# Routing the first 20 of 32 token tiles inside the attention stage ahead of each expert stage

## What is computed

```python
x = x + jnp.tanh(g_xattn[0]) * _L0_xattn_ref(_layernorm(x), ctx, ...)        # softmax attention, 8 heads
x = x + jnp.tanh(g_ffn[0])   * _L0_ffn_ref(_layernorm(x), ...)               # 8 experts, 2 per token, hidden 128
x = x + jnp.tanh(g_xattn[1]) * _L1_xattn_ref(_layernorm(x), ctx, ctx, ...)   # linear attention, 16 heads
x = x + jnp.tanh(g_ffn[1])   * _L1_ffn_ref(_layernorm(x), ...)               # a causal block, 32 heads, then
#   h = _rms(x, ff_ln_w); topv, topi = top_k(h @ wg, 4); gate = softmax(topv)  16 experts, 4 per token, hidden 256
#   y_e = (silu(h @ w1[e]) * (h @ w3[e])) @ w2[e];  x + sum over the chosen e of gate_e * y_e
```

## Time and profile before

| | us |
|---|---|
| median of 3 runs | 3075.64 |
| lowest, highest | 3073.47, 3088.97 |
| profiled execution | 3069.99 |
| its span | 3068.2 |
| its granted TensorE clock, mean share of full speed | 0.86 |
| busy in the span: TensorE, VectorE, ScalarE, GpSimd | 2334.5, 1909.9, 1086.7, 1091.4 |

### The profile page before, as it was taken

The page is one execution under the profiler, slowest core; times in us unless marked ns, Lnnn a source line. Parts: engine busy times, 40 slices in busy tenths (PEclk is TensorE's granted clock), DMA queues, the critical chain, the costliest instruction groups (busy, mean ns, idle before and its releaser), DMA issues. The chain is left out here.

```text
span 3068.2 us, 57408 instructions
## 1 busy us (share of the span) xinstructions
PE 2334.5 (76%) x19856; PEld 1800.8 (59%) x19856; DVE 1909.9 (62%) x3797; ACT 1086.7 (35%) x2118; POOL 1091.4 (36%) x1088
## 2 busy tenths in 40 slices
PE   4888899863782598993788898889886316999991
PEld 3455555443671487882576677667675315888770
DVE  4788788634453477774677867777775612444574
ACT  1566666521340232322333333333332202333330
POOL 2455455325325000000444443434442476000366
PEclk9898878655896799996999999899998557999995
DMA  5555655223566211103332232232223344333575
GB/s 104 112 134 126 126 131 117 44 79 99 161 183 182 90 35 52 38 27 104 77 76 62 62 78 64 62 75 66 56 73 102 117 156 149 99 99 99 179 232 158
DMA packets 251153, 313.43 MB, mean 102 GB/s; under 512 B 43648, under 2 KB 205568, under 8 KB 249728
## 3 DMA queue, kind: packets, MB, share of 16 engines
q1 hardware_dynamic: 190272, 220.09, 26.9%
q0 software_dynamic: 26624, 58.79, 7.3%
q10 hardware_dynamic: 33984, 30.95, 3.0%
HBM read 126.93 MB, written 98.30 MB: 73 GB/s over the span
## 5 line engine op out<-in xcount | busy, mean ns | idle before, releaser
L1655 POOL TENSOR_TENSOR ca_qk<-ca_qk,ca_q_swap 128x512 f32<-128x512 f32 x160 | 233.3, 1458 | 504.8 <-DVE ca_q_swap L1799 504.8
L317 DVE TENSOR_REDUCE soft_top<-soft_pa 128x4 fp32r<-128x1024 f32 x256 | 311.7, 1218 | 125.0 <-PE soft_pa L387 124.7
L738 POOL DMA_INDIRECT moe_yg<-moe_ys_rows,moe_slot_id x192 | 193.4, 1007 | 474.6 <-DMA moe_ys_rows<-moe_ys 364.1
L237 ACT ACTIVATE soft_prob<-soft_pb 128x1024 f32<-128x1024 f32 x256 | 262.0, 1023 | 230.2 <-PE soft_pb L371 229.9
L726 POOL DMA_INDIRECT moe_rows<-moe_hn,moe_slot_id x192 | 200.8, 1046 | 123.5 <-DVE moe_slot_id L911 65.5
L1870 PE MATMUL ca_pp<-ca_ht_hi,ca_w_hi 128*128 128x512 f32 x320 | 151.4, 473 | 97.5 <-ACT ca_q_f L1691 76.2
L1057 PE MATMUL moe_pgu<-moe_w_hi,moe_xt_hi 128*128 x472 | 192.8, 409 | 31.4 <-DVE moe_xt_lo L971 28.3
L1073 PE MATMUL moe_py<-moe_w_d,moe_at 128*128 x788 | 211.8, 384 | 0.0
L1691 ACT ACTIVATE ca_q_f<-ca_pp 128x512 f32<-128x512 f32 x160 | 94.9, 593 | 308.6 <-PE ca_pp L1870 301.1
L976 DVE TENSOR_TENSOR moe_act_f<-moe_silu,moe_pgu 128x256 f32<-128x256 f32 (+1 forms) x236 | 88.7, 376 | 172.7 <-ACT moe_silu L791 171.5
L971 DVE TENSOR_TENSOR moe_xt_lo<-moe_pt,moe_xt_hi 128x256 fp32r<-128x256 f32 x236 | 99.9, 423 | 138.9 <-ACT moe_xt_hi L786 138.7
(11 more groups left out here) (246 smaller groups left out, 6402.8 us busy)
## 6 DMA issues: line engine op xcount, KB each, us to landing
ca_q_swap<-ca_q_f SPq DMA_DIRECT2D x640, 64.0 KB, 2.0
moe_xs<-moe_rows SPq DMA_DIRECT2D x236, 128.0 KB, 2.0
moe_ys_rows<-moe_ys ACTq DMA_DIRECT2D x236, 128.0 KB
soft_rep<-soft_parts SPq DMA_DIRECT2D x384, 64.0 KB
moe_rows<-soft_blank SPq DMA_DIRECT2D x27, 768.0 KB
moe_hn<-scratch SPq DMA_DIRECT2D x16, 512.0 KB, 6.6
moe_xd<-scratch SPq DMA_DIRECT2D x64, 128.0 KB, 2.7
ca_vs<-ca_v SPq DMA_DIRECT2D x16, 512.0 KB
```

Source lines behind the costliest of these rows:

```text
L237: act.activation(prob[:, k % 4, :, :], p_b[:].rearrange("p (h s) -> p h s", h=2), ACT.Exp).then_inc(prob_ready, 1)
L317: dve.tensor_reduce(heads[:, j:j + 2, :, g], p_a[:].rearrange("p (h c s) -> p h c s", h=2, c=HALF), AX, ALU.max).then_inc(a_done, 1)
L738: pool.indirect_dma_start(out=yg[:, t % 2, k, :], out_offset=None, in_=ys_rows[h], in_offset=bass.IndirectOffsetOnAxis(ap=slot_id[:, t, k: ...
L1655: pool.tensor_tensor(qk[:, u % 2, m, :], qk[:, u % 2, m, :], q_swap[:, p % 2, :], ALU.add).then_inc(qk_ready, 1)
```

## The change

MOE_TILES = (20, 12) replaces COUNT = (24, 8). A new class `Router` holds the routing of one part, with a method for each engine's share. Part 0's twenty tiles are routed in the attention stage ahead, one tile after the other in softmax attention and chunk by chunk in causal attention: `spread` (VectorE, statistics), `root` (GpSimd), `scale` (VectorE; ScalarE in causal attention), `turn` (TensorE, transposes) and `keep_turned` (ScalarE), `grade` (TensorE, router products) and `keep_scores` (ScalarE), `choose` (VectorE). When all twenty are graded, `tally`, `rank`, `keep_ranks`, `place`, `map_blocks`, `keep_map`, `exps` and `weigh` run once, and `send` issues the scatters, 6 a pass in softmax attention from pass 28 on (40 in all) and 5 a step in causal attention from step 50 on (80 in all). Slots, weights and block experts go through DRAM to the expert stage (`leave`, `finish`), which routes the other twelve tiles itself and makes the low parts of weights in between. The norm's weight is folded into the router and, for the second stage, into the experts' high and low parts instead of the rows. TensorE's blocks wait for the tables as well; part 0's first block has no scatter to wait for. Blocks: 47 + 31 = 78 and 95 + 63 = 158.

Causal attention keeps `ht_hi`/`ht_lo`, `v`/`vs` and `ot_hi`/`ot_lo` once instead of twice: values are projected in places 0 and 1 of their own chunk, and ScalarE overwrites `ot_hi` only when the output products of the step before have been made. In softmax attention `xo` has four buffers instead of two.

The core of the diff:

```diff
+MOE_TILES = (20, 12)
...
+class Router:
...
+    def load(self, sp):
...
+    def spread(self, dve, g, row):
+        stats, mv, var = self.stats, self.mv, self.var
+        for t in range(self.GRP):
+            dve.bn_stats(stats[:, t, :], row(self.GRP * g + t)).then_inc(self.stat, self.stat_ticks.one())
...
+        for t in range(self.GRP):
+            dve.bn_aggr(mv[:, t, :], stats[:, t, :]).then_inc(self.stat, self.stat_ticks.one())
...
+    def root(self, pool, g):
...
+        pool.tensor_tensor(self.rstd[:], self.var[:], self.half_neg[:], ALU.pow).then_inc(self.rstd_ready, 1)
...
+    def scale(self, eng, g, row):
...
+        for i in range(self.GRP):
...
+    def turn(self, pe, first, tiles, out, ident):
+        pe.wait_ge(self.row_ready, first + tiles)
+        for t in range(tiles):
+            for k in range(self.KC):
+                mm = pe.transpose(out[:, t * DIM + k * PART:t * DIM + (k + 1) * PART],
+                                  self.rows[:, first + t, k * PART:(k + 1) * PART], ident)
...
+    def keep_turned(self, act, n, src, ht):
...
+    def grade(self, pe, g, tiles, out, ht):
...
+                mm = pe.matmul(out[:, t * self.EXPERTS:(t + 1) * self.EXPERTS], ht[:, t * DIM + k * PART:t * DIM + (k + 1) * PART],
+                               self.router[:, k, :], start=(k == 0), stop=(k == self.KC - 1))
...
+    def keep_scores(self, act, g, tiles, src):
...
+    def choose(self, dve, first, tiles, graded):
...
+            dve.max(top8[:, t, :], self.score[:, t, 0:E]).then_inc(route, ticks.one())
...
+            dve.match_replace(self.left[:, t, :], top8[:, t, :], self.score[:, t, :], MARK).then_inc(route, ticks.one())
...
+    def tally(self, dve):
...
+    def rank(self, pe, out):
...
+    def keep_ranks(self, act, src):
...
+    def place(self, dve):
...
+    def map_blocks(self, pe, out, ident):
...
+    def exps(self, act, stretches):
...
+    def weigh(self, dve):
...
+    def send(self, pool, first, last):
+        to = self.c["moe_rows"][self.h]
+        if first == 0:
+            pool.wait_ge(self.idx_ready, 1)
+        for n in range(first, min(last, self.n * self.TOP)):
+            t, k = divmod(n, self.TOP)
+            pool.indirect_dma_start(
+                out=to, out_offset=bass.IndirectOffsetOnAxis(ap=self.slot[:, t, k:k + 1], axis=0),
+                in_=self.rows[:, t, :], in_offset=None, bounds_check=self.blocks * PART - 1, oob_is_err=False
+            ).then_inc(self.sent, 16)
+    def tables(self, nc):
...
+    def leave(self, sp):
...
+    def finish(self, sp):
+        sp.wait_ge(self.saved, 48)
+        sp.wait_ge(self.sent, 16 * self.n * self.TOP)
...
-CLEARS = (19, 8)
+CLEARS = (16, 11)
...
-    LOAD, RING = 4, 16
+    LOAD, RING, KEEP = 4, 16, 4
+    ROUTED, STRETCH, SENDS = MOE_TILES[0], 4, 6
...
-        y, xo = sb("y", [PART, 2, T]), sb("xo", [PART, 2, T])
+        y, xo = sb("y", [PART, 2, T]), sb("xo", [PART, KEEP, T])
...
+        RANK = ROUTED + 6
...
+                route.leave(sp)
...
+                        past(pool, route.row_ready, min(t - KEEP + 1, ROUTED))
...
+                    if routed(i - 4):
+                        route.root(pool, i - 4)
...
+                    if i > RANK + 1:
+                        if i == RANK + 2:
+                            pool.wait_ge(cleared[0], 16 * CLEARS[0])
+                        route.send(pool, SENDS * (i - RANK - 2), SENDS * (i - RANK - 1))
+                route.send(pool, SENDS * (TILES + 1 - RANK), 2 * ROUTED)
...
+                    if routed(i - 6):
+                        route.keep_scores(act, i - 6, 1, p_x[0][:, T:T + 8])
...
+                    if routed(i - 5):
+                        route.keep_turned(act, i - 5, p_x[0][:, 0:T], turned[:])
+                    if i == RANK:
+                        route.keep_ranks(act, p_x[0])
+                        route.exps(act, ROUTED // STRETCH)
+                    if i == RANK + 1:
+                        route.keep_map(act, p_x[0])
...
+                    if routed(i - 4):
+                        dve.wait_ge(xo_ready, i - 3)
+                        route.spread(dve, i - 4, lambda t: xo[:, t % KEEP, :])
                     maxima(i, 1)
...
                     maxima(i, 6)
+                    if routed(i - 4):
+                        route.scale(dve, i - 4, lambda t: xo[:, t % KEEP, :])
                     maxima(i, 7)
+                    if routed(i - 6) and (i - 5) % STRETCH == 0:
+                        route.choose(dve, i - 5 - STRETCH, STRETCH, i - 5)
+                    if i == RANK - 1:
+                        route.tally(dve)
+                    if i == RANK + 1:
+                        route.place(dve)
+                    if i == RANK + 3:
+                        route.weigh(dve)
...
                     values(i - 1, 3)
+                    if routed(i - 6):
+                        route.grade(pe, i - 6, 1, p_x[0][:, T:T + 8], turned)
...
                     score(i, 7)
+                    if routed(i - 5) or i in (RANK, RANK + 1):
...
+                    if routed(i - 5):
+                        route.turn(pe, i - 5, 1, p_x[0], ident_f[:])
+                    if i == RANK:
+                        route.rank(pe, p_x[0])
+                    if i == RANK + 1:
+                        route.map_blocks(pe, p_x[0], ident_f)
                     values(i, 2)
...
-    COUNT = (24, 8)
+    COUNT = MOE_TILES
...
+        new = slice(FIRST[1], TILES)
+        route = Router(nc, st, name, name, 1, c, EXPERTS, TOP, norm, GRP, slot_id[:, new, :], wk[:, new, :], expert_of[:, START[1]:], x_new)
...
+                for dst, src in zip((slot_id[:, 0:COUNT[0], :], wk[:, 0:COUNT[0], :], expert_of[:, 0:BLOCKS[0]]), c[name + "_tables"]):
...
-                    if n == 0:
-                        sp.wait_ge(sent[h], 16 * COUNT[h] * TOP)
+                    if b == START[1]:
+                        sp.wait_ge(route.sent, 16 * NEW * TOP)
...
+                route.send(pool, 0, NEW * TOP)
+                pool.wait_ge(table_in, 48)
+                pool.wait_ge(route.sent, 16 * NEW * TOP)
...
+                high(0)
+                high(1)
+                route.keep_ranks(act, p_gu[0])
+                high(2)
+                high(3)
+                route.keep_map(act, p_at[0])
+                route.exps(act, GROUPS)
+                for e in range(4, EXPERTS):
+                    high(e)
...
+                for g in range(GROUPS):
...
+                    route.choose(dve, GRP * g, GRP, g + 1)
+                route.tally(dve)
+                low(0)
+                low(1)
+                route.place(dve)
+                low(2)
+                low(3)
+                route.weigh(dve)
+                for e in range(4, EXPERTS):
+                    low(e)
+                if norm == "layer":
...
+                pe.wait_ge(const_in, 32)
+                for g in range(GROUPS):
+                    for i in range(2):
+                        past(pe, route.ht_ready, 2 * (g - 1) + i + 1)
+                        route.turn(pe, GRP * g + 2 * i, 2, p_t[i], ident[:])
+                    past(pe, route.score_out, g - 1)
+                    route.grade(pe, g, GRP, p_y[g % 2], ht)
+                route.rank(pe, p_gu[0])
+                route.map_blocks(pe, p_at[0], ident)
                 pe.wait_ge(wlo_ready, EXPERTS)
                 pe.wait_ge(down_in, 16 * EXPERTS)
-                pe.wait_ge(expert_ready, PARTS)
+                pe.wait_ge(table_in, 48)
...
-        ht_hi, ht_lo = (sb(n, [PART, 2, KC, CHUNK], fp32r) for n in ("ht_hi", "ht_lo"))
+        ht_hi, ht_lo = (sb(n, [PART, KC, CHUNK], fp32r) for n in ("ht_hi", "ht_lo"))
...
-        v, vs = (sb(n, [PART, 2, TPC, KVHEADS * HD]) for n in ("v", "vs"))
+        v, vs = (sb(n, [PART, TPC, KVHEADS * HD]) for n in ("v", "vs"))
...
-        ot_hi, ot_lo = (sb(n, [PART, 2, RQ, 2 * PART], fp32r) for n in ("ot_hi", "ot_lo"))
+        ot_hi, ot_lo = (sb(n, [PART, RQ, 2 * PART], fp32r) for n in ("ot_hi", "ot_lo"))
+        route = Router(nc, st, "ca", "moe1", 0, c, 16, 4, "rms", TPC)
...
+        ROUTED = MOE_TILES[0] // TPC
+        SENDS = 5
...
+        def routing(n, place):
+            ch, j = step_of(n)
+            return ch - 1 if j == place and 0 <= ch - 1 < ROUTED else None
...
+        RANK = SPC * (ROUTED + 1)
...
+                    r = routing(n, 5)
+                    if r is not None:
+                        route.root(pool, r)
...
+                    if n > RANK + 1:
+                        route.send(pool, SENDS * (n - RANK - 2), SENDS * (n - RANK - 1))
+                route.send(pool, SENDS * (STEPS + 2 - RANK - 2), 4 * MOE_TILES[0])
...
-                            past(act, y_ready, n - 2)
...
+                            past(act, y_ready, n - 1)
...
+                    r = routing(n, 5)
+                    if r is not None:
+                        route.scale(act, r, routed_row(r))
+                    r = routing(n, 6)
```

(46 more changed lines are left out.)

## The result

The changed kernel takes 3064.56 us (median of 6 runs, 3062.95 to 3073.06), and its ratio to the kernel before is 0.9958 (95% interval 0.9941 to 0.9975): faster by 0.4%, about 13 us, where I had forecast 24 us, 0.8%. The profiled execution took 3064.46 us, its span is 3062.7. The sign was right, the gain about half.

A forecast was written before the change was run, and what follows sets the result against it. Bound: serial expert openings (score, rank, scatter, load), and attention stages where TensorE and VectorE are late in turns. Softmax +60, first experts -66, causal +78, second experts -96: -24 us, median 3052 us, own range 3025 to 3078, overall 2985 to 3112.

The forecast's parts named there:

- Openings: Starts of the two expert stages before their first blocks: shorter by 69 us (129.3 to 60) and 104 us (to 103).
- Sums at the end: GpSimd's serial fetches behind the expert blocks: +8 us in the second stage, +3 us in the first.
- Softmax scatters: Sixteen scatters behind GpSimd's last product in softmax attention, 21 us, plus 3 us of that product's lateness: 24 us.
- Softmax iterations: Softmax attention: spread and choose add 1.25 us to each of 20 iterations, TensorE's work nothing: 25 us.
- upper bound of 45: Upper end for the work inserted into softmax iterations, with everything serial: 45 us.
- Single ot buffers: Causal attention: ScalarE's copy must wait for the previous step's output products: +15 us, between 0 and 30.
- Routed chunks: Causal attention: per-chunk routing work on VectorE and TensorE, 6.1 us in each of five chunks: 30 us (15 to 45).
- Ranking: Causal attention: rank, place and weigh once at full clock, 4.8 + 2 + 8.2: 15 us (8 to 20).
- Rival B: Insertions fall into idle time of both attention stages, saving 50 of the 138 us added: 3002 us; chance 0.25.
- Rival C: GpSimd becomes the bound of causal steps, scatters costing 1654 + 300 ns beside VectorE's products: 3100 us; chance 0.18.
- Rival D: Openings instead wait for low halves and down weights behind VectorE's ranking, 83 and 128 us: 3100 us; chance 0.12.
- The row against the page: Earlier trace: a scatter took 4.93 us beside VectorE weight subtractions, though the Trainium skill's rule implies no hold-up.

The follow-up runs named there:

- no_pe: Changed kernel without TensorE's transposes and router products (and ScalarE's keeping of them) in softmax attention; ScalarE copies eight features as scores: softmax stage 726.6 us against 740.2.
- no_dve: Changed kernel without VectorE's spread and scale and GpSimd's root in softmax attention; ScalarE copies the rows: softmax stage 727.7 us against 740.2.
- neither: Changed kernel with both TensorE's and VectorE's per-tile routing work left out of softmax attention: softmax stage 706.5 us against 740.2.
- single_buf: Kernel before with only the single ht, v, vs and ot buffers and moved values' products, nothing routed early: causal stage 949.1 us against 945.4.
- late_rank: Changed kernel with softmax attention and first expert stage as before, causal ranking one step later, six scatters a step: 3135.43 us, ratio 0.994 to before.

## Why the prediction was right in sign and about double in size

- Openings, right. -69 and -104 against -67.3 and -111. The first block waits for down weights and low halves, as said. The 7 us more in the second: the low halves were done 78 us after its start, not 82, and the sixteen down weights took SyncE 9.71 us to issue, not the 14.67 of the earlier trace rows.
- Sums at the end, right: +8 against +7.3, 48 fetches for 41; +3 against +0.9.
- Softmax scatters, right: 24 against 24.0. Its ranking: 11 against 12 (means of 84 and 72 in that phase).
- Softmax iterations, wrong: 25 against 42 (37 in 21 iterations, 5 in the next three; means of the repeated kernels). The step that failed is "of that I take nothing, since TensorE waits for the peaks' DMA right there". no_pe, no_dve and neither put TensorE's term at 11 to 15 us. An idle gap whose end is another engine's or a DMA's work, which itself stands in the same chain, moves with the chain and covers nothing. Spread and scale, 17 in my sum, cost 18 to 21; choose, 8, is in the 7 to 10 that neither keeps, with ScalarE's copies. The second thing at nothing in my sum is the granted clock, 0.77 instead of 0.86: by the estimate above 13 to 16 us, which lie inside these numbers. My upper bound of 45 would have held it all. (The 15.7 us that I gave for an iteration at full clock was a misreading: at 1.00 it took 16.97.)
- Causal attention: 78 against 82.2 (87 by repeated stages), from errors that cancel. Single ot buffers 15, measured 0 to 4, the moved values among it: VectorE's 18.2 us of the earlier trace rows was a sign of slack, which I read and then priced all the same. Start +3, measured -3 to -6, since the first values moved out of it. Routed chunks 30, measured 33 (35 by the means of the kernels). Ranking 15, measured 29 (139.0 without scatters, against 110). Step by step against single_buf the changed kernel is 14.2 us longer in step 48, 7.0 in step 49 (place) and 7.4 in step 51 (weigh). The first is the term that was mis-sized: 4.8 for ranks that took 8.9, 6.0 of them L241's work at full clock, and nothing for the 4.55 us in which TensorE waits for VectorE's tally. Scatters 15, measured 16.7.
- Linear attention, no term: -4.7, and in the eight kernels with early softmax routing 387.7 to 393.2, without it 391.7 to 401.2. It is not explained; the stage's code is the same.
- Rival B (insertions fall into idle time) is refuted in both stages, which grew by 77 and 87 and not by 50 less than my 138. Rival C's price did not come about; its mechanism showed at six scatters a step. Rival D is refuted by the openings of 62 and 96. The row against the page held in the second opening only: there a scatter again took 5.50 us beside eight weight subtractions of VectorE. These are the timelines of GpSimd and VectorE of the changed kernel, beside the earlier trace rows:

```profile
2504.11 5.50 POOL L326 DMA_INDIRECT moe_rows<-moe_x_new,moe_slot_id  x1 [0.30 <-issue]
...
2503.39 5.37 DVE L1119 SCALAR_TENSOR_TENSOR moe_w_lo<-moe_raw,moe_r_norm_w,moe_w_hi 128x512 fp32r<-128x512 f32 x8
```

  It repeats in the eleven kernels with this stage, 5.50 to 5.62 us. In the attention stages 120 scatters took 0.99 to 1.0 us on the mean and 1.46 at most, among VectorE's shorter runs of products with two inputs. So, for the Trainium skill's rule ("SBUF — State Buffer", Who interferes with whom), this trace disagrees beside such a row of subtractions; elsewhere no row decides.
- The profiled execution of before was a quick one: 3069.99 us, against runs of 3063 to 3097 in all on the ordinary chips (but for one of 5414.1, which is left out). Its own sum says -5.5, the ratio -0.42%, 13 us. With the repeated stages my -24 is off by +17 in softmax attention, +9 in causal attention, -6 in the second opening and -5 in linear attention, which makes -9: most of the miss is the softmax iterations.

## What to carry to other kernels

Work moved from a serial opening into a pipelined stage must be priced on every engine of the chain that sets the iteration; a wait counts as cover only if what ends it lies outside that chain. Judge each place of a change by itself: here one of two halves brought everything, and the halves are told apart by running each alone. A single profiled execution was good for a phase to 2% here, and once to 3% only, so read a term of 5 us from phases that repeat.

## What the runs showed of the hardware

- The small fp32 products of the ranking follow the clock in full: 38 of them took 6.02 us at a granted clock of 1.00 (late_rank), 7.45 at 0.81 (changed kernel) and 8.31 at 0.72 (no_pe), and each time the part at half clock counts half.
- After a stop of 4.55 us TensorE ranked at 0.50 at first; where it came to the ranks without a stop (late_rank) the clock was 1.00.
- The granted clock of a stretch fell when work was added to it: softmax iterations at 0.86 before, 0.77 after, 0.85 with TensorE's and VectorE's routing left out.
- A scatter of GpSimd lasted as long as the row of VectorE subtractions beside it: 5.50 us beside eight of 5.37 in all, where it otherwise takes 0.97 to 1.0.
- Chips differ beyond the clock: on one, the kernel before takes 3152 us instead of some 3080, with standstills of ScalarE of up to 27 us in the expert stages.
